# Attention results of two tiles per unit, and the next tile's row maximum ahead of the unit's division and turning on VectorE

## What is computed

```python
x = x + attn(layernorm(x))        # window of 32 keys, 16 heads of 8
x = x + ffn(layernorm(x))

# attn
qkv    = x @ W_qkv + b_qkv
scores = einsum('bnid,bnjd->bnij', q, k) / sqrt(8)   # masked outside the window
out    = einsum('bnij,bnjd->bnid', softmax(scores), v)
return out @ W_out + b_out
# ffn: top-1 routed expert (7 of them, or none), times 2 and its probability,
#      plus a shared expert; hidden size 512, SiLU gate
```

## Time and profile before

| | |
|---|---|
| median of 3 runs | 367.31 us (366.27 to 370.47) |
| profiled execution | 367.33 us |
| its span | 365.6 us |
| TensorE busy, whole span | 330.0 us (90%) |
| VectorE busy | 225.6 us (62%) |
| ScalarE busy | 176.4 us (48%) |
| GpSimd busy | 174.9 us (48%) |
| mean granted TensorE clock | 0.973 |

### The profile page before, as it was taken

How to read it: one execution, slowest core, us unless ns; L and a number is a source line. 1 busy time by engine, 2 the same in 40 slices (tenths; PEclk the granted TensorE clock), 3 DMA queues, 4 the chain that set the end, 5 groups by cost and what they waited for, 6 DMA issues and landing times. The chain is left out here.

```text
span 365.6 us, 12604 instructions
## 1 busy us (share of the span) xinstructions
PE 330.0 (90%) x5014; PEld 260.7 (71%) x5014; DVE 225.6 (62%) x539; ACT 176.4 (48%) x313; POOL 174.9 (48%) x256
## 2 busy tenths in 40 slices
PE   8788999899999898997967999979999999999980
PEld 8545665565656555885855888868898999989970
DVE  4966997788988978779442333333555455554540
ACT  1646666567666575663221222214455554555530
POOL 6652455464557566692674444462333333333331
PEclk9989999999999999999889999998999999999996
DMA  8965333334433321000121111213222232222200
GB/s 207 357 219 149 90 109 98 97 105 129 133 101 100 102 44 32 2 2 0 37 86 56 67 61 60 88 43 81 77 66 65 69 73 71 67 67 69 74 5 0
DMA packets 40426, 30.66 MB, mean 84 GB/s; under 512 B 5792, under 2 KB 36772, under 8 KB 40370
## 3 DMA queue, kind: packets, MB, share of 16 engines
q1 hardware_dynamic: 36800, 23.17, 23.0%
q0 software_dynamic: 2880, 6.43, 5.0%
q10 hardware_dynamic: 690, 0.26, 0.4%
HBM read 13.72 MB, written 11.95 MB: 70 GB/s over the span
## 5 line engine op out<-in xcount | busy, mean ns | idle before, releaser
L599 POOL DMA_INDIRECT out<-y,tok_u x38 | 37.4, 984 | 72.8 <-DVE y L1199 72.8
L1214 DVE SCALAR_TENSOR_TENSOR Pr<-psS,xs,PT 128x256 f32<-128x256 f32 x76 | 33.3, 480 | 47.6 <-PE psS L1549 47.3
L881 DVE TENSOR_REDUCE row_max<-psS 128x16 fp32r<-128x1024 f32 x32 | 39.1, 1224 | 16.3 <-PE psS L1274 16.1
L1025 DVE TENSOR_TENSOR hT<-psS,PT 128x512 f32<-128x512 f32 x32 | 22.1, 690 | 41.4 <-PE psO L1436 17.1
L768 ACT ACTIVATE PT<-psS 128x512 f32<-128x512 f32 x32 | 19.2, 599 | 58.0 <-PE psS L1424 44.6
L1565 PEld LDWEIGHTS psB<-down_sb,Pr 128*128 128x128 f32 x304 | 40.2, 193 | 4.3 <-issue 1.0
L917 DVE STREAM_TRANSPOSE PT<-Pr 128x1024 f32<-128x1024 f32 x32 | 39.6, 1236 | 2.4 <-ACT Pr L671 2.2
L1565 PE MATMUL psB<-down_sb,Pr 128*128 x304 | 40.3, 276 | 0.8 <-ACT Pr L805 0.8
L428 POOL TENSOR_TENSOR rows<-rows,proj 128x128 f32<-128x128 f32 x31 | 14.2, 458 | 54.9 <-ACT proj L677 52.3
L1303 PEld LDWEIGHTS psO<-VD,PT 128*32 128x32 f32 x2048 | 22.3, 109 | 21.7 <-issue 21.1
L1274 PE MATMUL psS<-Kx,Qx 64*32 64x256 f32 x1024 | 35.1, 384 | 0.8 <-issue 0.8
(11 more groups left out here) (202 smaller groups left out, 730.8 us busy)
## 6 DMA issues: line engine op xcount, KB each, us to landing
sorted_rows<-pad_row SPq DMA_DIRECT2D x19, 264.0 KB
VD<-V SPq DMA_DIRECT2D x120, 36.0 KB, 2.4
xs<-sorted_rows SPq DMA_DIRECT2D x38, 66.0 KB, 2.0
base<-sorted_rows SPq DMA_DIRECT2D x38, 64.0 KB, 1.8
rows<-in_L_attn_x SPq DMA_DIRECT2D x8, 256.0 KB, 5.8
gate_sb<-in_L_ffn_w_gate SPq DMA_DIRECT2D x1, 1792.0 KB, 10.3
up_sb<-in_L_ffn_w_up SPq DMA_DIRECT2D x1, 1792.0 KB, 14.7
down_sb<-in_L_ffn_w_down SPq DMA_DIRECT2D x7, 256.0 KB, 3.4
```

The costliest lines, as they stand in the source:

```text
L599: pool.indirect_dma_start(out=out_list, out_offset=bass.IndirectOffsetOnAxis(tok_u[:, r : r + 1], 0), in_=y[:, r, :], in_offset=None, boun ...
L881: nc.vector.tensor_reduce(row_max[:, k % 2, :], s, AX.X, ALU.max).then_inc(max_done, 1)
L1214: nc.vector.scalar_tensor_tensor(out=hs[:, r % 2, h], in0=psS[:, r % 2, h], scalar=xs[:, q, GATE : GATE + 1], in1=sg[:, r % 2, h], op0=ALU ...
```

## The change

Tiles are joined in units: 17 of them, units 0 to 14 of two tiles, and units 15 and 16 of one each (tiles 30 and 31). The weighed values of both tiles of a unit stand in one `psO` bank (columns 0 to 287), units taking turns between the banks. Per unit there is one reciprocal, one division, one turning, one copy of the projection and one residual, each over both tiles; `On`, `OT`, `proj` and `rden` are one buffer of double width. The projection is two matmuls into columns 0 to 255 of the bank, over the weighed values, once they are divided. TensorE's step keeps its order, but the projection stands only in the steps of a unit's first tile, and is that of the unit before. In VectorE's `tile` the maximum of tile g+2 stands right behind the turning of g's probabilities; the output of the unit before follows it in steps with even g (and in the last one), the moments of two tiles in steps with odd g.

```diff
+    UNITS = NT // 2 + 1
+    def unit_of(b, k):
+        g = b * TPB + k
+        return g // 2 + (g == NT - 1)
+    def tiles_of(u):
+        return 2 if u < UNITS - 2 else 1
+    def first_tile(u):
+        return NT - 1 if u == UNITS - 1 else 2 * u
...
-        On = sb("On", [P, 2, D])
-        OT = sb("OT", [P, 2, D])
-        proj = sb("proj", [P, 2, D])
+        On = sb("On", [P, 2 * D])
+        OT = sb("OT", [P, 2 * D])
+        proj = sb("proj", [P, 2 * D])
...
+            def evict_proj(u):
+                n = tiles_of(u) * D
+                act.wait_ge(op_done, u + 1)
+                if u > 0:
+                    act.wait_ge(res_done, u)
+                nc.scalar.copy(proj[:, 0:n], psO[:, (u + 1) % 2, 0:n]).then_inc(proj_ready, 1)
...
+            def heads_sums(u):
+                g, n = first_tile(u), tiles_of(u)
+                dve.wait_ge(pv_done, g + n)
+                if u > 0:
+                    dve.wait_ge(on_done, u)
+                r = rden[:, 0 : n * NH].rearrange("q (h j) -> q h j", j=n * NJ)
+                nc.vector.reciprocal(r, heads_of(u)[:, :, 0 : n * NJ, HD]).then_inc(rden_done, 1)
...
                 turn_probs(b, k, first=first)
-                if k > 0:
-                    output(b, k - 1, first=first)
-                elif not first:
-                    output(b - 1, TPB - 1)
-                if k > 1:
-                    moments_after(b, k - 2)
-                elif not first:
-                    moments_after(b - 1, k + TPB - 2)
                 if k + 2 < TPB:
                     find_max(b, k + 2, first=first)
                 elif not last:
                     find_max(b + 1, k + 2 - TPB)
+                if u > 0 and (k % 2 == 0 or tiles_of(u) == 1):
+                    output(u - 1)
+                if k % 2 == 1 and u > 0:
+                    moments_after((b * TPB + k) // 2 - 1)
...
+                u = unit_of(b, k)
+                if u >= 2 and b * TPB + k == first_tile(u):
+                    pe.wait_ge(on_done, u - 1)
+                    pe.wait_ge(proj_ready, u - 1)
...
+            def project(u):
+                pe.wait_ge(ot_done, u + 1)
+                for t in range(tiles_of(u)):
+                    w = slice(t * D, (t + 1) * D)
+                    last = mm(psO[:, (u + 1) % 2, w], OT[:, w], wout_sb[:, :], start=True, stop=True)
+                last.then_inc(op_done, 1)
...
                 weigh_values(b, k, first=edge == "first")
-                if k > 0:
-                    project(b, k - 1)
-                elif edge != "first":
-                    project(b - 1, TPB - 1)
+                u = unit_of(b, k)
+                if u > 0 and b * TPB + k == first_tile(u):
+                    project(u - 1)
```

More of the change, by code:

```diff
@@ L422, in add_bias, with residual @@
                 pool.tensor_tensor(xb, xb, attn_bias[:, :, :].to_broadcast([P, TPB, D]), ALU.add).then_inc(xb_done, 1)
-            def residual(g):
-                pool.wait_ge(proj_ready, g + 1)
+            def residual(u):
+                pool.wait_ge(proj_ready, u + 1)
+                g, n = first_tile(u), tiles_of(u)
                 pool.wait_ge(xb_done, g // TPB + 1)
-                xk = x_all[:, g, :]
-                pool.tensor_tensor(xk, xk, proj[:, g % 2, :], ALU.add).then_inc(res_done, 1)
+                xk = x_all[:, g : g + n, :]
+                pool.tensor_tensor(
+                    xk, xk, proj[:, 0 : n * D].rearrange("p (t d) -> p t d", d=D), ALU.add
+                ).then_inc(res_done, 1)
             gate_flat = gate_sb[:, :, :].rearrange("p e h -> p (e h)")
@@ L519, in _ @@
             EARLY = 5 * TPB
[L520 to L524, removed]
+            for u in range(EARLY // 2):
+                b, half = divmod(u, 2)
+                residual(u)
+                for low in range(2):
+                    split(u, low)
+                if half == 0 and b + 3 < B:
                     normalise(b + 3)
-                if k == 3 and b + 2 < B:
+                if half == 1 and b + 2 < B:
                     add_bias(b + 2)
-            residual(EARLY)
+            residual(EARLY // 2)
             moments(0, G1)
-            residual(EARLY + 1)
             deviations(0, G1 // 2)
-            residual(EARLY + 2)
             deviations(G1 // 2, G1)
             shifts(0, G1)
-            residual(EARLY + 3)
+            residual(EARLY // 2 + 1)
             add_bias(B - 1)
-            for b in range(3):
-                residual(EARLY + 4 + b)
+            for b in range(2):
                 normalise_rows(b, 1)
-            residual(G2 - 1)
+            residual(EARLY // 2 + 2)
+            normalise_rows(2, 1)
+            residual(G2 // 2 - 1)
             first_parts()
             moments(G1, G2)
-            residual(G2)
             deviations(G1, G2)
             shifts(G1, G2)
-            residual(G2 + 1)
+            residual(G2 // 2)
             normalise_rows(5, 2)
-            residual(G2 + 2)
+            residual(UNITS - 2)
             def last_deviations(lo, hi):
@@ L693, in step @@
                     exponentials(*here, first=first is True and k == 0)
-                if k > 0:
-                    evict_proj(b, k - 1, first=first is True)
-                elif first is not True:
-                    evict_proj(b - 1, TPB - 1)
+                if k % 2 == 0 and b + k > 0:
+                    evict_proj(unit_of(b, k) - 1)
             def normalise_rows(b, group):
@@ L917, in turn_probs, with heads_of @@
                 nc.vector.transpose(PT[:, k % 2, :], Pr[:, k % 2, :]).then_inc(pt_done, 1)
[L919 to L928, removed]
+            def heads_of(u):
+                return psO[:, (u + 1) % 2, 0 : NH // NJ * UVW].rearrange("q (h j v) -> q h j v", j=2 * NJ, v=VW)
@@ new lines, in heads_sums, with divide_heads @@
+            def heads_sums(u):
+                g, n = first_tile(u), tiles_of(u)
+                dve.wait_ge(pv_done, g + n)
[3 more added lines that the diff above has]
+                nc.vector.reciprocal(r, heads_of(u)[:, :, 0 : n * NJ, HD]).then_inc(rden_done, 1)
+            def divide_heads(u):
+                n = tiles_of(u)
+                r = rden[:, 0 : n * NH].rearrange("q (h j) -> q h j", j=n * NJ)
+                dve.wait_ge(rden_done, u + 1)
+                if u > 0:
+                    dve.wait_ge(ot_done, u)
@@ L929, in divide_heads, with turn_heads @@
                 nc.vector.tensor_tensor(
-                    On[:, k % 2, :].rearrange("q (j h d) -> q h j d", j=NJ, d=HD), o[:, :, :, 0:HD],
-                    r.unsqueeze(3).to_broadcast([P, NH // NJ, NJ, HD]), ALU.mult,
+                    On[:, 0 : n * D].rearrange("q (j h d) -> q h j d", j=n * NJ, d=HD),
+                    heads_of(u)[:, :, 0 : n * NJ, 0:HD],
+                    r.unsqueeze(3).to_broadcast([P, NH // NJ, n * NJ, HD]), ALU.mult,
                 ).then_inc(on_done, 1)
[L934 to L938, removed]
+            def turn_heads(u):
+                n = tiles_of(u)
+                dve.wait_ge(on_done, u + 1)
+                if u > 0:
+                    dve.wait_ge(op_done, u)
+                nc.vector.transpose(OT[:, 0 : n * D], On[:, 0 : n * D]).then_inc(ot_done, 1)
@@ L944, in moments, with output, moments_after @@
                 ).then_inc(st2_done, 1)
[L946 to L953, removed]
+            def output(u):
+                heads_sums(u)
+                divide_heads(u)
+                turn_heads(u)
+            def moments_after(u):
+                dve.wait_ge(res_done, u + 1)
+                for g in range(first_tile(u), first_tile(u) + tiles_of(u)):
+                    moments(*divmod(g, TPB))
             def tile(b, k, first=False, last=False):
+                u = unit_of(b, k)
                 turn_probs(b, k, first=first)
-                if k > 0:
-                    output(b, k - 1, first=first)
-                elif not first:
-                    output(b - 1, TPB - 1)
-                if k > 1:
-                    moments_after(b, k - 2)
-                elif not first:
-                    moments_after(b - 1, k + TPB - 2)
                 if k + 2 < TPB:
@@ L980, in _ @@
             batch(B - 1, last=True)
-            output(B - 1, TPB - 1)
+            output(UNITS - 1)
             def aggregate(k):
@@ L987, in last_residual @@
             def last_residual():
-                dve.wait_ge(op_done, NT)
+                dve.wait_ge(op_done, UNITS)
                 dve.wait_ge(xb_done, B)
                 x_last = x_all[:, NT - 1, :]
-                nc.vector.tensor_tensor(x_last, x_last, psO[:, (NT - 1) % 2, OPC : OPC + D], ALU.add).then_inc(res_done, 1)
-                dve.wait_ge(res_done, NT)
+                nc.vector.tensor_tensor(x_last, x_last, psO[:, UNITS % 2, 0:D], ALU.add).then_inc(res_done, 1)
+                dve.wait_ge(res_done, UNITS)
                 moments(B - 1, TPB - 1)
@@ L1139, in _ @@
             aggregate(1)
-            moments_after(B - 1, TPB - 2)
```

(3 more changed lines are left out.)

30 lines of the change are left out of this document (9 added, 21 removed).

## The result

The changed kernel takes 403.83 us (median of four runs, 402.58 to 405.57), the kernel before 367.55 in the same comparison: a ratio of 1.105, 95% interval 1.098 to 1.111. The forecast was 388, range 381 to 397. The profiled execution took 404.46 us with a span of 402.7, against 367.33 and 365.6 before.

What follows compares the result with a forecast made beforehand. TensorE was taken to set the pace, VectorE's loop just under it. Longer steps from the projection's wait +23.3 us, covered stalls -4.1, tiles 28 to 31 +1.8: +21.0 on 367.33 gives 388 us, range 381 to 397.

Steps and rivals of the forecast that it cites:

- the loop of scores, maximum and shift: VectorE's loop beside TensorE in the attention: 3.30 us alone, 0.3 under TensorE's step of 3.62 us.
- The pair's operations: Reciprocal, division and turning over two tiles on VectorE: 0.27 + 0.46 + 0.44 = 1.17 us, bounds 0.89 and 1.78.
- the slope: Price of width on VectorE from a small and a large operation: 1.03 to 1.04 ns a column.
- cold weights: Projection's weights not preloaded after its wait: 0 to 0.2 us, taken as 0.10.
- The clean steps: Attention steps free of stalls, k=0 to 3: 5.36, 3.33, 5.78, 3.30 us; 17.77 a batch instead of 14.19.
- The term of the stalls: Stalls between the masks of steps 2 and 28, 7.6 us: 4.1 covered by the projection's wait, 3.5 staying.
- the sum for a clock of 1.00: Forecast time between the masks of steps 2 and 28 at full clock: 99.19 + 23.3 - 4.1 = 118.4 us.
- the first rival: Clock falls at each of 14 projection waits, 1.72 us each: 24 us more, 412 us; chance 0.08.
- the rest: Outside those marks only tiles 28 to 31 were to lengthen, +1.8 us together; later work moves as a block.
- The argument against the rival: Clock stayed at 1.00 from 136 to 139 us despite a 1.51 us gap; some 7 us dense work surrounds each gap.
- Nothing behind the projection was late: Rival: queries' copy, residual or moments lose 1 us a pair beyond their slack, 14 us more, 402 us; chance 0.06.
- The case without a wait: Rival: output ready in time, so no projection wait in even steps; 1.7 us saved, 365.6 us; chance 0.05.

## Why the prediction was wrong

*Right.* TensorE sets the pace, and the loop of scores, maximum and shift lies just under it. The maximum gained nothing by its new place. The projection stood for 1.9 us (1.86 forecast) in each even step. The pair's operations: reciprocal to division 0.39 us (0.27 forecast), division to turning 0.45 (0.46), turning 0.45 (0.44):

```profile
101.10 1.23 DVE L893 TENSOR_REDUCE row_max<-psS 128x16 fp32r<-128x1024 f32 x1 [0.66 <-PE psS L1293]
...
102.24 0.35 DVE L940 RECIPROCAL rden<-psO 128x32 f32<-128x32 f32 x1
...
102.63 0.42 DVE L948 TENSOR_TENSOR On<-psO,rden 128x256 f32<-128x256 f32 x1
...
103.08 0.45 DVE L959 STREAM_TRANSPOSE OT<-On 128x256 f32<-128x256 f32 x1
```

Only the reciprocal is off: the slope was taken from a multiplication, and 16 more columns cost 0.13 us, not 0.02. That makes up the 0.10 that I had added for cold weights, of which nothing shows. The clean steps came out at 5.40, 3.43, 5.82 and 3.39 (5.36, 3.33, 5.78, 3.30): 18.04 a batch, 0.27 over the sum.

*Off in size, without effect on the sum.* The term of the stalls: I let 3.5 of 7.6 us stay. With TensorE kept busy 117.6 us were measured, some 1 us above the clean steps; in the changed kernel practically none are left. This term and the longer odd steps partly cancel, so it is in part luck that the sum for a clock of 1.00 (118.4) is met within 1 us.

*The step that failed* is the clock, which the sum left at nothing and the first rival had at a chance of 0.08. The rival had the mechanism and nearly the price, 1.72 us a fall; the falls cost 1.31 to 1.64 us, ten of them in 13 pairs, 15.7 us. 388 + 15.7 is 403.7, and 403.8 was measured. That it fits so closely is luck too: without the falls the stretch between the marks grew by 17.4 us, where 19.2 were forecast, and the rest by 4.0 instead of 1.8.

The argument against the rival rested on one gap, 1.51 us with a clock of 1.00 behind it, and on the dense work around each gap. The runs show that dense work does not keep the clock up: the waits of 1.91 us, with some 7 us of work between them, were followed by a fall in ten of 13 cases and, on another chip, in nine of 13. And the trace of the kernel before had more to say. Besides the gap of 1.83 us and one of 2.87 us at 189.31, this one stands in its expert tiles, with 4 us of dense work ahead of it:

```profile
245.54 0.30 PE L1528 MATMUL psA<-ident,xs 128*128 128x128 f32 x1 [1.50 <-DVE xsT L1134]
```
```profile
245.00:250.00 5.00, 4.08 (x13) 3.15 (x14) 1.77 (x8) 2.02 (x5) 1.91 (x2) 0.67 0.12 38
```

From 30 us on there are four gaps of 1.5 us or more, and three of them were followed by a fall. Read together, they make this case the likelier one, with a range up to 412.

The length of a gap does not settle it alone. The wait of 1.81 to 1.84 us of the earlier trace rows (`down_sb`<-`hT`) is in all 13 traces of this case; a fall follows it in six and none in seven, and of the two traces of the changed kernel one is in each group. The 2.41 us above had none. What decides in a single case stays open.

The section of the Trainium skill's page "TensorE: Matmul & The Clock Gate" on a second failure mode tells of a clock that swings where TensorE idles briefly between groups of matmuls. The changed kernel did that: its clock is 0.83 to 0.91 over stretches of 20 us. The traces agree with the section for the recurring waits of 1.91 us and show no fall at those of 1.77 us and under in the attention from 36 us on.

*The rivals.* Nothing behind the projection was late: the weighings in even steps did not hold it up. The case without a wait did not arise. The range ended at 397 because it left the clock out. It also left out one of its own bounds: with none of the stalls covered, 4.1 us more, it would have ended at 401, still short of the result.

## What to carry to other kernels

Ahead of an edit that moves work on one engine, read what the waiting instruction on the other engine has queued behind it: the output was allowed to be late, and the projection stood in front of the work that the next maximum needs; moved behind it, most of the loss was gone. Where an edit opens a gap on TensorE, price it twice, once as time and once as clock, and take the chance of a fall from all gaps of about that length in the trace, not from the one row that suits. Widening an operation that is not the bound gained nothing here.

## What the runs showed of the hardware

At a wait that recurs in each even step of the attention (from 36 us on) the clock of TensorE stayed at 2.4 GHz with gaps of 1.44 to 1.58 us, and fell for a while to 1.2 GHz behind most gaps of 1.91 us (10 of 13 on one chip, 9 of 13 on another), at a price of 1.3 to 1.6 us each. Four small matmuls in the gap, which took 0.33 us off it, made the difference of 13.6 us between the marks on one chip. With every step interrupted for 1.54 us and TensorE busy for 71% of the time (59.35 of 84) the clock did not fall.

None of these lengths is a threshold. Gaps of 1.71 to 1.77 us, five in one run, and a single one of 2.41 us had no fall in the attention; one of 1.50 us in the expert tiles had one; the same wait of 1.81 to 1.84 us had one in 6 of 13 traces. Why three of the 13 gaps on one chip and four on another had no effect stays open as well.

The chips used differ by 10 us for the kernel before. For the changed kernel 13.4 of 16.9 us lie behind the mask of step 28, in the last steps of the attention and the stages after it.
